# Channel mix of a routed two-layer network on one Trainium2 core: one 128-row matmul a chunk, or two 64-row matmuls

## What is computed

```python
# layer 0: mix the 64 channels of each sample with the 64x64 matrix of its condition
y  = einsum('bct,bcd->bdt', x, cond_weights[cond])            # the channel mix
r0 = y @ W_base.T + b_base                                    # 1024 x 1024
r0 += top-2 routed low-rank part: ((y @ A.T) * route_w) @ B   # 8 experts of rank 16
x1 = x + r0
# layer 1: each sample takes one of 8 adapters (1024 x 1024), then a soft-routed low-rank part
z  = x1 @ weight[adapter].T
out = x1 + 32/16 * (((z @ A1.T) * scores) @ B1),  scores = 8 * softmax(z @ Wr.T + br)
```

## Time and profile before

| | us |
|---|---|
| three runs: lowest, median, highest | 807.42, 807.62, 807.78 |
| profiled execution, its own time | 808.33 |
| its span | 806.6 |
| TensorE matmul busy in the span | 756.8 (94%) |
| VectorE, ScalarE, GpSimd busy | 463.7, 234.9, 309.8 |
| mean granted TensorE clock | 0.984 of full speed |

### The profile page before, as it was taken

How to read it: one execution, slowest core, us unless ns; L and a number is a source line. 1 busy time by engine, 2 the same in 40 slices (tenths; PEclk the granted TensorE clock), 3 DMA queues, 4 the chain that set the end, 5 groups by cost and what they waited for, 6 DMA issues and landing times.

```text
span 806.6 us, 14497 instructions
## 1 busy us (share of the span) xinstructions
PE 756.8 (94%) x4768; PEld 734.3 (91%) x4768; DVE 463.7 (57%) x1257; ACT 234.9 (29%) x491; POOL 309.8 (38%) x174
## 2 busy tenths in 40 slices
PE   2786888999999999999999999999999999999993
PEld 2676888999999999999999999999999999999993
DVE  5798564455555555555555555555555555555553
ACT  3333342322222222222222222222222222222220
POOL 6998001433333333333333333333333333333322
PEclk9999899999999999999999999999999999999997
DMA  8776663011111111111111111111111111111001
GB/s 278 254 253 210 206 207 106 0 53 54 53 53 53 52 52 52 52 52 52 50 43 45 46 51 52 52 52 47 42 44 49 52 52 52 52 52 52 27 27 52
DMA packets 16678, 62.17 MB, mean 77 GB/s; under 512 B 2068, under 2 KB 2068, under 8 KB 16660
## 3 DMA queue, kind: packets, MB, share of 16 engines
q1 hardware_dynamic: 15122, 55.09, 18.8%
q0 software_dynamic: 1232, 6.33, 2.4%
q10 hardware_dynamic: 306, 0.53, 0.3%
HBM read 45.16 MB, written 16.78 MB: 77 GB/s over the span
## 4 chain that ended last, share of the span: by engine, by line
PE 89%; DVE 6%; issue 1%; DMA 1%; ACT 1%; POOLq 1%; DVEq 0%; SPq 0%; ACTq 0%; POOL 0%
PE main_ps L283 19%; PE main_ps L282 19%; PE main_ps L284 19%; PE main_ps L296 8%; PE turn_ps L314 7%; PE low_ps L360 4%; PE turn_ps L360 4%; PE turn_ps L348 4%; DVE yT L596 3%; PE out_ps L282 2%; PE out_ps L284 2%; PE out_ps L283 2%; DVE x1T L596 1%; DMA ring<-in_w 1%; DVE x_lo L596 1%
## 5 line engine op out<-in xcount | busy, mean ns | idle before, releaser
L282 PE MATMUL main_ps<-w_lo,yT 128*128 128x386 f32 (+1 forms) x768 | 271.2, 353 | 0.0
L283 PE MATMUL main_ps<-w_hi,yT 128*128 128x386 f32 (+1 forms) x768 | 260.8, 340 | 0.0
L284 PE MATMUL main_ps<-w_hi,yT 128*128 128x386 f32 (+1 forms) x768 | 260.3, 339 | 0.0
L809 POOL TENSOR_TENSOR adapter<-folded,adapter 128x1088 fp32r<-128x1088 f32 x64 | 160.8, 2537 | 17.7 <-issue 17.7
L805 POOL TENSOR_TENSOR wait_col<-zero_cols 128x1 f32<-128x1 f32 x32 | 6.2, 195 | 368.3 <-ACT adapter L471 368.3
L283 PEld LDWEIGHTS main_ps<-w_hi,yT 128*128 128x128 f32 x768 | 145.2, 189 | 0.0
L282 PEld LDWEIGHTS main_ps<-w_lo,yT 128*128 128x128 f32 x768 | 144.9, 189 | 0.1
L284 PEld LDWEIGHTS main_ps<-w_hi,yT 128*128 128x128 f32 x768 | 144.7, 188 | 0.0
L798 POOL TENSOR_TENSOR ring<-ring,bias_rows 128x1024 f32<-128x1024 f32 x32 | 76.3, 2385 | 84.7 <-PE turn_ps L314 84.7
L461 ACT CAST yT<-turn_ps 128x512 fp32r<-128x512 f32 x64 | 37.6, 588 | 196.3 <-PE turn_ps L314 196.3
L628 DVE COPY hg<-main_ps 128x136 f32<-128x136 f32 x32 | 9.6, 300 | 143.8 <-PE main_ps L284 143.8
(11 more groups left out here) (109 smaller groups left out, 1050.2 us busy)
## 6 DMA issues: line engine op xcount, KB each, us to landing
ring<-in_w SPq DMA_DIRECT2D x40, 512.0 KB, 4.2
ring<-in_x SPq DMA_DIRECT2D x32, 512.0 KB, 3.3
out<-ring SPq DMA_DIRECT2D x32, 512.0 KB, 2.6
y<-in_w POOLq DMA_DIRECT2D x5, 464.0 KB, 5.5
bias_rows<-in_w POOLq DMA_DIRECT2D x5, 464.0 KB, 4.0
folded<-in_ag SPq DMA_DIRECT2D x1, 544.0 KB, 5.5
cond_table<-in_w_cond ACTq DMA_DIRECT2D x2, 256.0 KB
y<-in_b POOLq DMA_DIRECT2D x1, 512.0 KB, 3.5
```

The lines of the kernel that those rows point to most:

```text
L282: pe.matmul(dst, st_hi, mv_lo, start=start, stop=False, skip_group_check=True)
L283: pe.matmul(dst, st_lo, mv_hi, start=False, stop=False, skip_group_check=True)
L284: return pe.matmul(dst, st_hi, mv_hi, start=False, stop=stop, skip_group_check=True)
L809: pool.tensor_tensor(adapter[:, :, b, 1, :], folded[:, bass.ds(e, 1), :, :].rearrange("p a k n -> p (a k) n"), adapter[:, :, b, 0, :], ALU ...
```

## The change

Each fp32 matmul of the mix over 128 rows is replaced by two over 64 rows: sample b has the rows b*64 to b*64+63 of the ring buffer as stationary side, its own 64 x 64 matrix (rows b*64 and on of `wc`, now 64 columns wide) as moving side, and the bank `turn_ps[b]` for all eight chunks. The two alternate, chunk by chunk. The whole mix of tile r+1 stands ahead of main group 0; nothing of it is left between group 0 and group 1. `yT` keeps its layout, so the copies out of the banks now write every second run of 64 columns. `wc` needs no zeros any more, and its memset is turned to another small tile to keep the semaphore's count.

```diff
-        wc = sb("wc", [P, P], F32)
+        wc = sb("wc", [P, CH], F32)
...
+        def mixed(b):
+            return turn_ps[b][:, :].rearrange("p (k t) -> p k t", k=KC)
+
+        def yT_part(r, part, b):
+            return yT[:, r % 2, part, :].rearrange("p (k s t) -> p k s t", k=KC, s=2)[:, :, b, :]
...
-            def make_yT(q, r, batch):
+            def make_yT(q, r):
                 later = not isinstance(q, int)
-                if batch == 0:
-                    pe.wait_ge(x_landed[r % RING], 16 * q + 16 * (r // RING + 1))
-                    pe.wait_ge(wc_done, 8 * q + 2 * r + 2)
-                    if r >= 3 or later:
-
-                        pe.wait_ge(lg_done, 8 * q + 2 * (r - 3) + 2)
-                for c in range(batch * KC // 2, (batch + 1) * KC // 2):
-                    mm = pe.matmul(turn_ps[batch][:, (c % 4) * P:(c % 4 + 1) * P],
-                                   ring[:, r % RING, c * P:(c + 1) * P], wc[:, :],
-                                   start=True, stop=True, skip_group_check=True)
-                mm.then_inc(yT_done, 1)
+                pe.wait_ge(x_landed[r % RING], 16 * q + 16 * (r // RING + 1))
+                pe.wait_ge(wc_done, 8 * q + 2 * r + 2)
+                if r >= 3 or later:
+                    pe.wait_ge(lg_done, 8 * q + 2 * (r - 3) + 2)
+
+
+                for c in range(KC):
+                    for b in range(2):
+                        half = slice(b * CH, (b + 1) * CH)
+                        mm = pe.matmul(turn_ps[b][:, c * CH:(c + 1) * CH],
+                                       ring[half, r % RING, c * P:(c + 1) * P], wc[half, :],
+                                       start=True, stop=True, skip_group_check=True)
+                        if c == KC - 1:
+                            mm.then_inc(yT_done, 1)
...
                 if ahead:
-                    make_yT(q, r + 1, 0)
+                    make_yT(q, r + 1)
                 first = isinstance(q, int) and r == 0
                 if l0:
                     pe.wait_ge(yT_lo_done, 8 * q + 2 * r + 2)
                     if not first:
                         pe.wait_ge(x1_done, 12 * q + 3 * (r - 1) + 1)
                     main(q, r, 0, 0, KC).then_inc(hg_done, 1)
-                if ahead:
-                    make_yT(q, r + 1, 1)
...
-            make_yT(0, 0, 0)
-            make_yT(0, 0, 1)
+            make_yT(0, 0)
...
-                    act.copy(wc[half, half], cond_table[half, bass.ds(no, 1), :].rearrange("p a n -> p (a n)")
+                    act.copy(wc[half, :], cond_table[half, bass.ds(no, 1), :].rearrange("p a n -> p (a n)")
...
-                    act.copy(yT[:, r % 2, 0, b * 512:(b + 1) * 512], turn_ps[b][:, :]).then_inc(yT_hi_done, 1)
+                    act.copy(yT_part(r, 0, b), mixed(b)).then_inc(yT_hi_done, 1)
...
-                    cols = slice(b * 512, (b + 1) * 512)
                     dve.wait_ge(yT_hi_done, 8 * q + 2 * r + b + 1)
-                    dve.tensor_tensor(yT[:, r % 2, 1, cols], turn_ps[b][:, :], yT[:, r % 2, 0, cols], ALU.subtract
+                    dve.tensor_tensor(yT_part(r, 1, b), mixed(b), yT_part(r, 0, b), ALU.subtract
                                       ).then_inc(yT_lo_done, 1)
...
-            pool.memset(wc[:, :], 0.0).then_inc(const_set, 2)
+            pool.memset(wait_col[:, :], 0.0).then_inc(const_set, 2)
```

## The result

| | before | after |
|---|---|---|
| median of the runs, us | 807.7 (807.42 to 809.55, 4 runs) | 825.44 (824.5 to 827.35, 4 runs) |
| ratio to before, 95% interval | | 1.0218, 1.0194 to 1.0242 |
| profiled execution: time, span | 808.33, 806.6 | 827.35, 825.6 |
| mean granted clock | 0.984 | 0.981 |

The change is 2.2% slower: 17.7 us between the medians, 19.0 us between the profiled executions. The forecast (820, range 809 to 880, slower with 0.80) named the side and the mechanism; its sum of 12.9 us was 4.8 us too small.

What follows compares the result with a forecast made beforehand. TensorE's own stream, and any new wait in it, was taken to bound the main loop. 808.33 + 0 (mix) + 7.2 (switches) + 5.7 (turn's wait) = 821.2, 820.5 for the median, stated as 820; range 809 to 880.

Steps and rivals of the forecast that it cites:

- The halves run side by side at the load's pace: In the mix, both 64-row halves overlap, 16 x 0.112 us a tile as now: 0 us.
- Rival (a): In the mix, 64-row loads queue one at a time: +57.3 us, 877.8 us; chance 0.24.
- (b): In the mix, only one of a matmul's two loads overlaps, three slots a chunk instead of two: +28.7, 849 us; chance 0.13.
- (c): In the mix, a 64-row load is short enough that 64 moving columns decide: -28.7, 791.8 us; chance 0.13.
- The switches: At the mix's borders, 64 changes between 128-row and 64-row work, one unhidden load of 0.112 us each: +7.2 us.
- bounds of 0 and 17.6: At the mix's borders, total switch cost in us: free below, 64 x 0.275 us above.
- the sign: First main matmul after the mix and first mix record after out_ps late by 0.1 to 0.3 us: shows the switches.
- the upper bound: Per switch at the mix's borders: last matmul running out, 0.163 us, plus load not hidden, 0.112 us; 17.6 us in all.
- a sign of being wrong: At the mix's borders, a switch over 0.3 us, or a mix time other than about 1.8 us, would refute the forecast.
- The turn waits for yT_low: At the turn of x1, yT_low stands behind copy_hg on DVE: +0.19 us in each of 30 tiles, +5.7 us.
- put this wait down to DVE: Load row's idle time ahead of the turn's load, 0.22 us a tile, would grow by about 0.2, attributed to DVE.
- The other edits: Earlier yT_high, strided yT writes, POOL's add_bias, waits ahead of the mix, wc copy and memset: each 0 us.

Runs made afterwards that it cites:

- experiment 3: Changed kernel with the mix's loops exchanged, all eight chunks of sample 0 and then all of sample 1: 913.61 us, ratio 1.1294.
- experiment 4: Changed kernel with each mix matmul over all 128 rows, still 64 moving columns, the other sample's rows of wc zero: 875.36 us, ratio 1.0819.
- experiment 7: Changed kernel with TURN_AT = 4 and every 64-row mix matmul but the first chunk's cut into two of 64 stationary columns: 797.24 us, ratio 0.986.
- the first experiment: Kernel before with its 128-row mix kept, but all of the mix ahead of main group 0: 813.13 us, ratio 1.0066.
- 6: Changed kernel with the mix cut into two blocks of four chunks, each behind one bank of make_out: 836.38 us, ratio 1.0345.
- 8: Changed kernel with twelve 386-column matmuls nobody reads, in TensorE's wait for the first tile's yT: 821.53 us, ratio 1.017.
- 2: Changed kernel with TURN_AT = 4, twelve main matmuls instead of nine between group 0 and the turn: 817.79 us, ratio 1.0109.
- 5: Kernel before with TURN_AT = 4, twelve main matmuls instead of nine ahead of the turn: 804.98 us, ratio 0.9961.
- experiment 9: As experiment 7, but first chunk also in quarters, mix's waits ahead of make_out's second bank, one unread matmul before the first mix: 789.49 us, ratio 0.9762.

## Why the prediction was right, and where it was short

*The halves run side by side at the load's pace (0 us).* Right. Pairs at 0.113 us after the change; experiment 3 shows that the alternation does it, experiments 4 and 7 that the load is what sets the pace. Rival (a), one load at a time, was a real alternative: with the loops exchanged it happens. Rivals (b) and (c) fell: there is no third slot, and a 64-row load isn't shorter. The 0.09 us that spoke for (c) was a mean: in the trace the second load of the turn starts 0.06 us after the first, the others 0.11 us apart. What shortens a load is fewer columns, as experiment 7 shows. The section "LDWEIGHTS" of the Trainium skill's page "TensorE: Matmul & The Clock Gate" says the same; the trace agrees: 0.112 us for 128 columns, with 64 rows or 128, and 0.058 for 64 columns with 64 rows.

*The switches (7.2 us).* This is the term that was mis-sized. I took one unhidden load for each switch, 0.225 us a tile. The runs show 0.325 (1.495 + 1.932 against 1.400 + 1.702), times 31 = 10.1 us, inside the bounds of 0 and 17.6. The mix starts 0.095 us later behind out_ps, and the main work behind it follows later by the rest, 0.23; the forecast had named 0.1 to 0.3 us as the sign. How the cost splits into a load not hidden and a matmul running out, the two parts of the upper bound, no run shows. Over 0.3 us a switch was named as a sign of being wrong; 0.325 is the price of two, entry and exit. The page "TensorEngine Tiling (Array Packing)" of the Trainium skill (section "Key Properties") calls this a drain; the trace agrees with the rule, the load row being idle for 0.37 us at each entry, though not with the whole of the 0.55 us a tile that I priced it at.

*The turn waits for yT_low (5.7 us).* Right in its mechanism: 0.19 us a tile forecast, 0.184 measured for the whole new order, 5.3 us in the first experiment's time. That the two are so close is in part luck. The wait after the change was forecast at 0.21 us and is that (a gap of 0.388 against 0.180 without a wait). The wait before was put at 0.02 and is 0.06 in the gap. So the wait grew by 0.15, and the 0.03 to 0.04 us that the forecast didn't have made up for it. I had also said that the profile would put this wait down to DVE; it puts it down to issue.

*The other edits (0).* Right: 590 and 681 ns for the strided copies, and POOL and ACT wait for others as before (POOL 416 us in all for ACT's adapter, where it was 368).

*What failed to appear in the sum.* The half clock at the start, 3.4 us. The forecast had no term for the clock at all, since the kernel before shows none of it there. 10.1 + 5.5 + 3.4 = 19.0 us, the difference of the two profiled executions. The medians differ by 17.7, of which the first two terms leave 2.1 for the clock. The three were tried apart: experiments 6, 1 and 8.

Open: why the clock falls. In the changed kernel the first mix has matmuls of 64 rows and 64 moving columns, and a wait follows. The profiles of the kernels whose mix has 64 moving columns (after, and 2, 3, 4, 6, 7, 9) show the fall there unless filled; those with the old mix (before, 1, 5) do not, one profile each. Experiment 4 has it with all 128 rows, so the halved rows aren't needed for it; whether the 64 moving columns are, or something else that the new first mixes share, wasn't tried.

## What to carry to other kernels

Halving a matmul's moving side is worth nothing while the load of its stationary side sets the pace; find that out from the distance of two loads, and cut the stationary columns first. Matmuls on separate rows or columns of the array do run side by side, if they are issued in turns (here each half of the rows had a bank of its own; one bank for both wasn't tried), but a passage from full-array work to such work and back costs 0.33 us here, so the block must save more than that. And when a step moves ahead of another, look at which engine's fixed order its consumer stands in: here yT_low stood behind copy_hg, the earlier mix hid nothing, and one constant (the place of the turn) was worth more than the order.

## What was not expected of the hardware

- How close work side by side stands, loads included: two loads start 7 ns apart and each holds its rows for 0.112 us; four start within 0.02 us, at 0.058 us a group. In experiment 9 a mix's 64 loads and 64 matmuls take 1.09 us together, 0.017 us a matmul.
- With one half of the array at work for 3.3 us, between full-array stretches and without any gap, the granted clock fell to half behind 23 of 29 mixes (experiment 3). The changed kernel and experiment 7, with both halves at work, keep the whole clock in the loop, and so does experiment 4, whose mix takes 3.5 us over all 128 rows.
- A change of shape inside 64-row work (64 x 128 to 64 x 64 columns) is a switch as well: 0.25 us a tile for its removal.
